# Scores of a tile in one run over four banks, in a fused adaLN block on one core

## The chip, the cores and the metric

One core of a Trainium2 chip runs the whole kernel, in one launch. The metric is the device time of an execution in microseconds: 976.61 us for the kernel before (median of 3 runs, 974.08 to 976.62). The core's engines each work through their own instructions in program order and meet at semaphores: TensorE (PE; its weight loads are PEld), VectorE (DVE), ScalarE (ACT), GpSimd (POOL) and SyncE (SP), which only issues DMAs here.

## What is computed

For x of 4 x 2048 tokens with 256 features (float32), with six modulation vectors per batch row from a small product:

```python
h = layernorm(x) * (1 + ca) + sa
q, k, v = phi(h @ Wq), phi(h @ Wk), h @ Wv     # phi = elu + 1, 16 heads of 16
S_t = S_{t-1} + k_t v_t^T ; z_t = z_{t-1} + k_t  # causal linear attention, a scan over tokens
x = x + ga * ((q_t S_t / max(q_t z_t, 1e-6)) @ Wo)
h = layernorm(x) * (1 + cb) + sb
x = x + gb * moe(h)   # 8 experts, top 2, capacity 1280 each, one shared silu layer of 512
```

## The kernel before, in words

The sequence is cut into 64 tiles of 128 tokens, four tiles to a group (16 groups). The attention phase is a software pipeline over slots, one tile to a slot (`slot_` of each engine; `run_slots` unrolls 8 slots to a loop body). Slot n handles tile n's scores, its state and its value products; the normalisation, the transpose and the out product of tile n-1; one quarter of the projections of the next group (q=0: transposes, q=1: Q, q=2: K, q=3: V, each of the last three in two halves, `stage1_qk` and `stage1_v`); and one step of the second layernorm and of the router for a group further back (q=0: transposes and logits, q=1: choice of experts, q=3: positions). q is the slot's place in its group. Every engine has its own order of these steps, written out by hand in its `slot_`; semaphores with running counts connect them.

Within one tile causal linear attention is a masked product. `scores` multiplies keys with queries, 32 rows (two heads, separated by a mask in QM) at a time: four row strips r = 0..3, each with two feature chunks cc. The scores of two strips (a pair) fill the tensor SCW, two PSUM banks of 512 columns, and DVE's `masked_scores` (L820) multiplies them with a triangle into Sm. The second pair uses the same two banks, so PE computes it (second call of `scores`) after DVE has read the first. PE's order in a slot (L1307 to L1360) is: scores of pair 0; logit rows, positions or h2 transposes, by q; `head_rows` (tile n-1's outputs transposed into bank MD); `key_rows` (keys transposed into bank MA); `from_state` (Q times the state, into OB); first half of stage 1; scores of pair 1; `attention_columns` (the normalised outputs An transposed into MA); `from_tile` part 0 (values times Sm, as column strips of 17 rows, adding to OB); `add_to_state`; second half of stage 1; `out_product` into MD; `from_tile` part 1. In a q=0 slot the logits stand before `from_tile` part 1 and `out_product`.

ACT's order in a slot (L656): OTs from OB of the last tile (L669), the masked queries of the next tile (L644), Kn from MA (L689), the first half of stage 1 (q=0: L582 drains both transposed halves; else L603 exp and L604 relu, or L652 for V), ATs from MA (L707), the layernorm rows (q=2 and q=3, L607), and the second half of stage 1. DVE's order (L964): mask of pair 0, `normalise_heads` (den, rden, An; L829 to L836), mask of pair 1, ATs' low part (L842), phi (L858) of the first half of stage 1, the state (L850), og = out product times ga (L1019), statistics; in q=1 phi of the second Q half and then the tails of both layernorms (L862 to L865), in q=2 phi of the second K half. Router steps of 0.2 to 0.7 us (`choose` in q=1, `place` in q=3) are put between these by `between`. POOL adds og to X (L491), applies the modulation in q=2 and q=3 (L459, L465), makes hT's low part in q=0 (L485) and sends the router's rows by indirect DMA (L475).

Projections, the out product and the expert products run as fp32r in three passes (`SPLIT`: high x high, high x low, low x high); for them w_o and ATs are kept as high and low parts. Scores, from_state, from_tile and the state run in full float32, where each matmul leaves two records in the trace.

Behind the attention phase (37 to 655 us of the span) stands a short end of the routing, and from 700 us on the expert phase, which uses SCW's two banks, MA and MD for its gate and down products and w_o's space for one of two XT buffers.

Of the kernel before, what the change touches and what calls it, by code (L numbers as in the profile page):

```python
# [21 lines left out]
P = 128  # L22
# [29 lines left out]
def adaln_block(nc, x, wqkv, wo, wr, wg, wd, c, wmod, out, xe, mod_rows):  # L52
    with ExitStack() as ctx:
# [24 lines left out]
        ATs = sb("ATs", [P, 2, DC, P], F32R)  # L78
        og = sb("og", [P, D])
        w_qkv = sb("w_qkv", [P, 2, DC, 3 * D], F32R)  # L80
        w_o = sb("w_o", [P, 2, DC, D], F32R)
# [62 lines left out]
        KS = sb("KS", [P, 2, DC, BW], F32R)  # L144
        w_d_lo = sb("w_d_lo", [P, FC, D], F32R)
# [11 lines left out]
        w_o_raw = Hf[:, DC * 3 * D:DC * 4 * D].rearrange("p (c n) -> p c n", c=DC)  # L157
# [16 lines left out]
              for a in (KS[:].rearrange("p k c n -> p (k c n)"), w_o[:].rearrange("p k c n -> p (k c n)"))]  # L174
# [46 lines left out]
        sc_full = sem("sc_full")  # L221
# [12 lines left out]
        at_hi = sem("at_hi")  # L234
        at_lo = sem("at_lo")
# [80 lines left out]
        def _(sp):  # L316
# [27 lines left out]
            sp.wait_ge(w_lo, 2)  # L344
# [206 lines left out]
        def _(act):  # L551
# [3 lines left out]
            for dst, src in ((w_qkv_raw, wqkv), (w_o_raw, wo), (w_r[:, :, 0:E], wr), (w_g_raw, wg)):  # L555
                act.dma_start(dst, src).then_inc(w_in, 16)
# [15 lines left out]
            for dst, src in ((w_qkv, w_qkv_raw), (w_o, w_o_raw)):  # L572
                act.activation(dst[:, 0], src, ACT.Copy).then_inc(w_hi, 1)
# [63 lines left out]
            def next_tile_queries(T, q, gp, tp, n):  # L637
# [3 lines left out]
                if n >= 1:  # L641
                    act.wait_ge(sc_full, 4 * T)
# [13 lines left out]
            def slot_(it, j, n):  # L656
# [47 lines left out]
                if tile_ok(n - 1):  # L704
                    act.wait_ge(at_full, T)
                    at_least(act, op_full, T - 1)
                    act.activation(ATs[:, 0].rearrange("p c i -> p (c i)"), MA[:, 0:D], ACT.Copy).then_inc(at_hi, 1)  # L707
# [76 lines left out]
        def _(dve):  # L784
# [5 lines left out]
            def early():  # L790

                for k, (dst, src) in enumerate(((w_qkv, w_qkv_raw), (w_o, w_o_raw))):
                    dve.wait_ge(w_hi, k + 1)
                    dve.tensor_tensor(dst[:, 1], src, dst[:, 0].bitcast(F32), ALU.subtract).then_inc(w_lo, 1)
# [15 lines left out]
                dve.wait_ge(w_hi, 3)  # L810
# [4 lines left out]
            def masked_scores(T, pair, tp, n):  # L815
                dve.wait_ge(sc_full, 4 * T + 2 * pair + 2)
                if pair == 0 and n >= 2:
# [3 lines left out]
                                  SCW[:].rearrange("p k (c w) -> p c k w", c=DC),  # L821
# [3 lines left out]
            def normalise_heads(T, between):  # L825

                on = MD[:].rearrange("p (h w) -> p h w", h=H)
# [10 lines left out]

            def attention_lo(T):

                dve.wait_ge(at_hi, T)
                dve.tensor_tensor(ATs[:, 1].rearrange("p c i -> p (c i)"), MA[:, 0:D],  # L842
                                  ATs[:, 0].rearrange("p c i -> p (c i)").bitcast(F32),
                                  ALU.subtract).then_inc(at_lo, 1)
# [119 lines left out]
            def slot_(it, j, n):  # L964
# [163 lines left out]
        def _(pe):  # L1128
# [17 lines left out]
            def scores(T, q, gp, tp, pair):  # L1146

                if isinstance(T, int) and T == 0 and pair == 0:
                    pe.wait_ge(gate_fix, 3)
                if pair == 0:  # L1150
                    pe.wait_ge(q_masked, 2 * T + 2)
                at_least(pe, sm_done, 2 * T + pair)
                last = [None, None]
                for cc in range(DC):
                    for k in range(2):
                        r = 2 * pair + k
                        rows = slice(32 * r, 32 * r + 32)
                        last[k] = mm(SC[k][:, cc * 2 * P:(cc + 1) * 2 * P], KT[rows, gp, cc, q * P:(q + 1) * P],  # L1158
                                     QM[rows, tp, :, cc, :], start=True, stop=True)
                for k in range(2):  # L1160
                    last[k].then_inc(sc_full, 1)

            def head_rows(T, q):

                pe.wait_ge(ot_done, T)
                at_least(pe, og_done, T - 1)
# [4 lines left out]
            def key_rows(T, q, gp):  # L1171
                at_least(pe, at_lo, T - 1)
# [12 lines left out]
            def from_tile(T, q, gp, tp, part):  # L1185

                pe.wait_ge(sm_done, 2 * T + 1 + part)
# [21 lines left out]
            def attention_columns(T, n):  # L1209
# [3 lines left out]
                else:  # L1213
                    pe.wait_ge(at_lo, T - 1)
# [24 lines left out]
            def stage1_qk(G, m):  # L1239
                N = G + 1  # L1240
                if isinstance(G, int) and N == 0 and m == 0:
                    pe.wait_ge(w_lo, 2)
# [23 lines left out]
            def h2_transposes(G, gn, hp):  # L1266
                pe.wait_ge(h2_done, 4 * (G - 1))
                if group_ok(gn):
# [25 lines left out]
            def positions(G, T, n):  # L1294
# [3 lines left out]
                at_least(pe, og_done, T - 1 if tile_ok(n - 2) else TILES)  # L1298
# [8 lines left out]
            def slot_(it, j, n):  # L1307
# [5 lines left out]
                if tile_ok(n):  # L1313
                    scores(T, q, gp, tp, 0)
# [142 lines left out]
```

## Time and profile before

| | |
|---|---|
| median of the runs | 976.61 us |
| the profiled execution | 978.2 us, its span 976.2 us |
| PE busy | 878.3 us (90%) |
| DVE busy | 652.8 us (67%) |
| ACT, POOL busy | 496.3 (51%), 514.9 us (53%) |
| slices 3 to 26 of 40, PE | nine tenths, PEclk 9 |

Times are microseconds from the start of the span. A row of the windows view is one stretch: its bounds, its length, then for PE, PEld, DVE, ACT and POOL the busy time and the number of instructions, then the granted clock of TensorE (1.00 is full), the DMA share and GB/s. A row of the groups by line is: line, engine, operation, output<-inputs, shapes, count; busy time of all together, mean ns of one; idle time ahead of them and what ended it. A row of the timeline is: start, duration, engine, line, operation, output<-inputs, shape and how many records were merged; in square brackets idle time before it and what ended it. A merged run of matmuls lasts until its last record has left the array, so the next run starts before it ends: PE's cost is read from start to start.

### The profile page before, as it was taken

To read this page: it belongs to the slowest core of one execution; us is meant where nothing else is said; L and a number is where in the kernel's file an instruction comes from. 1 tells how busy PE (TensorE), PEld (TensorE's weight loads), DVE (VectorE), ACT (ScalarE), POOL (GpSimd) and SP (SyncE) were. 2 spreads that over 40 slices of the span, in tenths; PEclk is the share of its full clock that TensorE was granted. 3 is DMA by queue.
4 is the path that set the end of the run, shared out by engine and by line. 5 is a ranking of instruction groups with operands and counts; after the bars stand their busy time and mean duration, and the time that the engine had idled before them with its cause. 6 is when DMAs were issued, how large, how long until landed. Compare 5 with 4: busy or idle time off the path is not lost. (4 is left out here: it accounts for less than half of the span.)

```text
span 976.2 us, 23383 instructions
## 1 busy us (share of the span) xinstructions
PE 878.3 (90%) x8232; PEld 736.6 (75%) x8232; DVE 652.8 (67%) x1869; ACT 496.3 (51%) x1002; POOL 514.9 (53%) x625
## 2 busy tenths in 40 slices
PE   4999999999999999999999999981099999999994
PEld 2777877777778777777777777761099999999994
DVE  4467587787877867778778787775056665665653
ACT  4555655655646555555565565432065555445541
POOL 3212445465554655556546555465625765566564
PEclk9899999999999999999999999995589999999997
DMA  9983012141231521302214112112156666666653
GB/s 318 335 272 97 16 31 110 23 131 66 66 116 13 130 86 43 127 31 82 78 21 96 40 37 60 33 39 64 53 148 147 143 131 141 144 138 141 129 110 43
DMA packets 70981, 98.36 MB, mean 101 GB/s; under 512 B 7794, under 2 KB 52850, under 8 KB 70792
## 3 DMA queue, kind: packets, MB, share of 16 engines
q1 hardware_dynamic: 37912, 52.09, 20.1%
q0 software_dynamic: 21760, 31.66, 14.6%
q10 hardware_dynamic: 11248, 13.81, 4.4%
q8 instruction: 37, 0.61, 0.3%
q14 instruction: 24, 0.20, 0.1%
HBM read 46.84 MB, written 63.36 MB: 113 GB/s over the span
## 5 line engine op out<-in xcount | busy, mean ns | idle before, releaser
L820 DVE TENSOR_TENSOR Sm<-SCW,tri 128x1024 f32<-128x1024 f32 x128 | 156.1, 1219 | 74.3 <-PE SCW L1158 74.3
L1158 PE MATMUL SCW<-QM,KT 32*128 32x256 f32 x1024 | 144.9, 400 | 10.5 <-DVE Sm L820 10.4
L475 POOL DMA_INDIRECT slot_rows<-Hrow,sloti x128 | 127.3, 994 | 45.1 <-issue 42.0
L533 POOL DMA_INDIRECT out<-EX,desti x80 | 126.6, 1583 | 29.6 <-issue 28.8
L491 POOL TENSOR_TENSOR X<-X,og 128x256 f32 (+1 forms) x64 | 47.3, 739 | 168.2 <-DVE og L1019 167.5
L1158 PEld LDWEIGHTS SCW<-QM,KT 32*128 32x128 f32 x1024 | 87.7, 184 | 45.8 <-issue 19.3
L1250 PE MATMUL PJ<-hT,w_qkv 128*128 128x512 f32 x384 | 106.9, 416 | 6.1 <-POOL hT L485 6.1
L485 POOL TENSOR_TENSOR hT<-N,hT 128x512 fp32r<-128x512 f32 x32 | 41.6, 1323 | 106.8 <-ACT hT L590 106.8
L603 ACT ACTIVATE EX<-PJ 128x512 f32<-128x512 f32 x64 | 38.2, 597 | 103.0 <-PE PJ L1250 103.0
L1250 PEld LDWEIGHTS PJ<-hT,w_qkv 128*128 128x128 f32 x384 | 69.6, 194 | 18.5 <-issue 6.3
L1191 PE MATMUL OB<-Sm,VA 128*17 128x128 f32 x2048 | 80.7, 275 | 0.0
L435 POOL TENSOR_TENSOR idle<-mhalf 128x1 f32<-128x1 f32 x100 | 33.2, 332 | 84.8 <-DVE EX L1103 59.2
L1019 DVE TENSOR_TENSOR og<-MD,MB 128x256 f32<-128x256 f32 x64 | 27.2, 424 | 67.8 <-PE MD L1224 67.8
L742 ACT ACTIVATE VA<-SCW 128x512 f32<-128x512 f32 x80 | 47.9, 598 | 40.9 <-PE SCW L1389 38.4
L1182 PE MATMUL OB<-QT,Sbd 128*128 128x128 f32 x512 | 67.6, 275 | 0.0
L1389 PE MATMUL SCW<-KS,w_g 128*128 128x256 f32 x480 | 63.2, 289 | 0.1
L1404 PE MATMUL MA<-w_qkv,QS 128*128 128x256 f32 x416 | 60.1, 281 | 3.0 <-DVE QS L1075 3.0
L1404 PE MATMUL MD<-w_qkv,hT 128*128 128x256 f32 x384 | 60.3, 281 | 2.5 <-DVE hT L1075 2.5
L1182 PEld LDWEIGHTS OB<-QT,Sbd 128*128 128x128 f32 x512 | 62.2, 192 | 0.0
L1389 PE MATMUL SCW<-w_o,w_g 128*128 128x256 f32 x480 | 62.2, 286 | 0.0
L1389 PEld LDWEIGHTS SCW<-KS,w_g 128*128 128x128 f32 x480 | 59.5, 194 | 0.5 <-DVE KS L1067 0.5
L1191 PEld LDWEIGHTS OB<-Sm,VA 128*17 128x17 f32 x2048 | 46.2, 97 | 17.6 <-issue 10.9
(191 smaller groups left out, 1996.3 us busy)
## 6 DMA issues: line engine op xcount, KB each, us to landing
Hrow<-slot_rows SPq DMA_DIRECT2D x32, 516.0 KB, 4.4
slot_rows<-erow ACTq DMA_DIRECT2D x1, 10400.0 KB, 53.1
X<-x SPq DMA_DIRECT2D x16, 512.0 KB, 4.3
out<-X SPq DMA_DIRECT2D x16, 512.0 KB, 3.0
Hrow<-mod_rows SPq DMA_DIRECT2D x16, 512.0 KB, 7.9
QT<-slot_rows SPq DMA_DIRECT2D x8, 516.0 KB, 3.7
slot_rows<-Hrow,sloti POOLq DMA_INDIRECT x128
N<-wd SPq DMA_DIRECT2D x4, 512.0 KB, 4.5
```

Of the source, the lines that this page charges most:

```text
L475: pool.indirect_dma_start(xe, bass.IndirectOffsetOnAxis(sloti[:, k, t:t + 1], 0), Hrow[:, 1 - gp, t, :], None, bounds_check=SLOTS - 1, oob ...
L485: pool.tensor_tensor(hT[:, 1, cidx, :], hT_raw[:, cidx, :], hT[:, 0, cidx, :].bitcast(F32), ALU.subtract).then_inc(h_lo, 1)
L491: pool.tensor_tensor(xt, xt, og[:], ALU.add).then_inc(x1_done, 1)
L533: pool.indirect_dma_start(out, bass.IndirectOffsetOnAxis(desti[s % 2][:, a:a + 1], 0), Ys[s % 2][:, a, :], None, bounds_check=TOK - 1, oob ...
L742: act.activation(hid_raw[s % 2][:, f, :], SC[hh].rearrange("p (f n) -> p f n", f=2), ACT.Silu).then_inc(silu_done, 1)
L820: dve.tensor_tensor(o.rearrange("p c (k w) -> p c k w", k=2), SCW[:].rearrange("p k (c w) -> p c k w", c=DC), tri[:].rearrange("p k i -> p ...
L1158: last[k] = mm(SC[k][:, cc * 2 * P:(cc + 1) * 2 * P], KT[rows, gp, cc, q * P:(q + 1) * P], QM[rows, tp, :, cc, :], start=True, stop=True)
L1182: mm(OB[:, i * P:(i + 1) * P], Sbd[:, 4 * i:4 * i + 4, :].rearrange("p h w -> p (h w)"), QT[:, gp, i // 2, q * P:(q + 1) * P], start=(i == ...
L1191: last = mm(OB[32 * a:32 * a + SW, i * P:(i + 1) * P], VA[:, gp, q, h, :], Sm[:, tp, h, :], start=False, stop=(part == 1), skip_group_chec ...
L1250: last = mm(PJ[m % 2][:], w_qkv[:, wp, cc, m * P:(m + 1) * P], hT[:, hp, cc, :], start=(cc + i == 0), stop=(cc == DC - 1 and i == len(SPLI ...
L1389: last = mm(SC[hh][:, (f % 2) * BW:(f % 2 + 1) * BW], w_g[:, wp, cc, f * P:(f + 1) * P], XT[par][:, xp, cc, :], start=(cc + i == 0), stop= ...
L1404: last = mm((MA, MD)[par][:, a * D:(a + 1) * D], hid[par][hp][:, f, a * P:(a + 1) * P], WD[k][wp][:, f, :], start=(f + i == 0), stop=(f == ...
```

## The change

SCW gets four banks: the first two are also MA and MD, the last two are SC[0] and SC[1]. `scores` runs once a slot, over all four strips; `masked_scores` is called twice at the head of DVE's slot. The transposes into MA and MD wait until the first masked pair has been read. The out product becomes one full float32 product (two matmuls) instead of six fp32r ones, so ATs and w_o lose their low parts; `attention_lo` goes, XT's second buffer is a new tensor VS, the router's positions move to PJ[1]. PE's slot is reordered. The core of the diff:

```diff
-        SCW = ctx.enter_context(nc.psum_tensor("SCW", [P, 2, 512], F32))
-        SC = [SCW[:, k, :] for k in range(2)]
+        SCW = ctx.enter_context(nc.psum_tensor("SCW", [P, 4, 512], F32))
+        MA, MD, *SC = (SCW[:, k, :] for k in range(4))
-        MA = ps("MA")
-        MD = ps("MD")
-        pos_ps = MD[:, 0:GT * E].rearrange("p (t e) -> p t e", t=GT)
+        pos_ps = PJ[1][:, 0:GT * E].rearrange("p (t e) -> p t e", t=GT)
...
-                act.activation(dst[:, 0], src, ACT.Copy).then_inc(w_hi, 1)
+            act.activation(w_qkv[:, 0], w_qkv_raw, ACT.Copy).then_inc(w_hi, 1)
...
                 if tile_ok(n):
                     masked_scores(T, 0, tp, n)
+                    masked_scores(T, 1, tp, n)
...
                 if tile_ok(n):
                     between()
-                    masked_scores(T, 1, tp, n)
                 between()
-                if tile_ok(n - 1):
-                    attention_lo(T)
                 between()
...
+            def scores(T, q, gp, tp):
+                pe.wait_ge(q_masked, 2 * T + 2)
+                at_least(pe, sm_done, 2 * T)
+                at_least(pe, og_done, T - 1)
+                at_least(pe, at_done, T - 1)
                 for cc in range(DC):
-                    for k in range(2):
+                    for r in range(4):
                         rows = slice(32 * r, 32 * r + 32)
+                        last = mm(SCW[:, r, cc * 2 * P:(cc + 1) * 2 * P], KT[rows, gp, cc, q * P:(q + 1) * P],
+                                  QM[rows, tp, :, cc, :], start=True, stop=True)
+                        if cc == DC - 1:
+                            last.then_inc(sc_full[r // 2], 1)
...
             def key_rows(T, q, gp):
-                at_least(pe, at_lo, T - 1)
+                pe.wait_ge(sm_done, 2 * T + 1)
...
             def out_product(T):
-                pe.wait_ge(at_lo, T)
+                pe.wait_ge(at_done, T)
                 for cc in range(DC):
-                    for i, (ap, wp) in enumerate(SPLIT):
-                        last = mm(MD[:, 0:D], ATs[:, ap, cc, :], w_o[:, wp, cc, :], start=(cc + i == 0),
-                                  stop=(cc == DC - 1 and i == len(SPLIT) - 1))
+                    last = mm(MD[:, 0:D], ATs[:, cc, :], w_o[:, cc, :], start=(cc == 0), stop=(cc == DC - 1))
```

`head_rows` waits for the first masked score of its slot too, `positions` for PJ[1] to be drained, `from_tile` part 0 in q=0 for the V projections to be drained. PE's slot after the change:

```python
                if tile_ok(n):
                    scores(T, q, gp, tp)
                ... # logit_rows (q=1), positions (q=3), h2_transposes (q=0), as before
                if tile_ok(n):
                    from_state(T, q, gp)
                if stage1:
                    ... # q=1: stage1_qk(G, 0); q=2: stage1_qk(G, 2); q=3: stage1_v(G, 0)
                if tile_ok(n - 1):
                    head_rows(T, n)
                if tile_ok(n):
                    key_rows(T, q, gp)
                    from_tile(T, G, q, gp, tp, 0)
                    add_to_state(T, q, gp, tp, j)
                if stage1 and q == 0:
                    stage1_transposes(G, gn)
                if tile_ok(n - 1):
                    attention_columns(T, n)
                if tile_ok(n):
                    from_tile(T, G, q, gp, tp, 1)
                if tile_ok(n - 1):
                    out_product(T)
                if stage1:
                    ... # q=1: stage1_qk(G, 1); q=2: stage1_qk(G, 3); q=3: stage1_v(G, 1)
                if q == 0 and group_ok(gn - 2):
                    logits(G, stage1)
```

The order of ACT's and DVE's other steps is not changed; ACT's copy of ATs now signals PE directly.

## Rows read from the trace of the kernel before

**Rows 1.** Windows view: the four slots of one group, q = 0 to 3.
```profile
306.23:315.31 9.08, 9.08 (x111) 7.30 (x107) 4.37 (x8) 6.49 (x13) 2.62 (x3) 1.00 0.00 0
315.31:324.89 9.58, 9.58 (x88) 7.28 (x87) 8.06 (x27) 3.82 (x9) 7.48 (x9) 1.00 0.53 193
324.89:335.31 10.42, 9.55 (x90) 7.19 (x87) 8.53 (x28) 6.37 (x15) 5.01 (x7) 1.00 0.66 117
335.31:345.60 10.29, 9.97 (x107) 8.16 (x104) 9.43 (x29) 5.72 (x14) 7.45 (x13) 1.00 0.04 9
```
**Rows 2.** Groups by line and shape: the column strips of `from_tile`, whole span.
```profile
L1191 PE MATMUL OB<-Sm,VA 128*17 128x128 f32 x2048 | 80.7, 275 | 0.0
```
**Rows 3.** Timeline of PE: one q=1 slot (its logit row left out).
```profile
315.31 1.13 PE L1158 MATMUL SCW<-QM,KT 32*128 32x256 f32 x8
...
316.53 0.60 PE L1168 MATMUL MD<-ident,OTs 128*128 128x128 f32 x4
316.97 0.38 PE L1174 MATMUL MA<-ident,KT 128*128 128x128 f32 x2
317.19 1.06 PE L1182 MATMUL OB<-QT,Sbd 128*128 128x128 f32 x8
318.00 1.65 PE L1250 MATMUL PJ<-hT,w_qkv 128*128 128x512 f32 x6
319.58 1.13 PE L1158 MATMUL SCW<-QM,KT 32*128 32x256 f32 x8
320.64 0.44 PE L1217 MATMUL MA<-ident,An 128*128 128x128 f32 x2
321.01 0.63 PE L1191 MATMUL OB<-Sm,VA 128*17 128x128 f32 x16
321.57 0.73 PE L1204 MATMUL SB<-VA,Kn 128*128 128x136 f32 x4
322.05 1.65 PE L1250 MATMUL PJ<-hT,w_qkv 128*128 128x512 f32 x6
323.54 0.87 PE L1224 MATMUL MD<-w_o,ATs 128*128 128x256 f32 x6
324.33 0.63 PE L1191 MATMUL OB<-Sm,VA 128*17 128x128 f32 x16
```
**Rows 4.** Timeline of PE: q=0's stage-1 transposes, q=2's second score run.
```profile
309.77 1.04 PE L1236 MATMUL PJ<-ident,N 128*128 128x128 f32 x8
...
330.00 1.13 PE L1158 MATMUL SCW<-QM,KT 32*128 32x256 f32 x8 [0.87 <-DVE Sm L820]
```
**Rows 5.** Timeline of ACT: drains and ATs in q=0, the drain behind q=1.
```profile
311.10 1.45 ACT L582 ACTIVATE N<-PJ,saca 128x512 f32<-128x512 f32 x2 [1.63 <-PE PJ L1236]
312.43 0.38 ACT L707 ACTIVATE ATs<-MA 128x256 fp32r<-128x256 f32 x1
...
323.74 0.60 ACT L603 ACTIVATE EX<-PJ 128x512 f32<-128x512 f32 x1 [2.23 <-PE PJ L1250]
324.23 0.59 ACT L604 ACTIVATE QT<-PJ 128x512 f32<-128x512 f32 x1
```
**Rows 6.** Timeline of DVE: from phi to mask to An, around q=2 and q=3.
```profile
325.52 0.69 DVE L858 SCALAR_TENSOR_TENSOR QT<-QT,EX 128x512 f32<-128x512 f32 x1
...
328.72 1.22 DVE L820 TENSOR_TENSOR Sm<-SCW,tri 128x1024 f32<-128x1024 f32 x1
...
330.35 0.42 DVE L836 TENSOR_TENSOR An<-MD,rden 128x256 f32<-128x256 f32 x1
...
335.53 1.22 DVE L858 SCALAR_TENSOR_TENSOR KT<-KT,EX 128x512 f32<-128x512 f32 x1
336.67 1.21 DVE L820 TENSOR_TENSOR Sm<-SCW,tri 128x1024 f32<-128x1024 f32 x1
...
340.70 0.41 DVE L836 TENSOR_TENSOR An<-MD,rden 128x256 f32<-128x256 f32 x1
```
**Rows 7.** Timeline of POOL: the add beside the phi at 335.53.
```profile
335.47 0.73 POOL L491 TENSOR_TENSOR X<-X,og 128x256 f32 x1 [4.97 <-DVE og L1019]
```

More of the change, by code:

```diff
@@ L77, in adaln_block @@
         An = sb("An", [P, H, DH])
-        ATs = sb("ATs", [P, 2, DC, P], F32R)
+        ATs = sb("ATs", [P, DC, P])
         og = sb("og", [P, D])
         w_qkv = sb("w_qkv", [P, 2, DC, 3 * D], F32R)
-        w_o = sb("w_o", [P, 2, DC, D], F32R)
+        w_o = sb("w_o", [P, DC, D])
         w_r = sb("w_r", [P, DC, 32])
@@ L173, in adaln_block @@
         XT = [a.rearrange("p (k c n) -> p k c n", k=2, c=DC)
-              for a in (KS[:].rearrange("p k c n -> p (k c n)"), w_o[:].rearrange("p k c n -> p (k c n)"))]
+              for a in (KS[:].rearrange("p k c n -> p (k c n)"), VS[:].rearrange("p k c n -> p (k c n)"))]
         Ys = [EXf[:, i * 512:(i + 1) * 512].rearrange("p (a n) -> p a n", a=2) for i in range(2)]
@@ L554, in _ @@
             act.wait_ge(wr_zero, 1)
-            for dst, src in ((w_qkv_raw, wqkv), (w_o_raw, wo), (w_r[:, :, 0:E], wr), (w_g_raw, wg)):
+            for dst, src in ((w_qkv_raw, wqkv), (w_o[:], wo), (w_r[:, :, 0:E], wr), (w_g_raw, wg)):
                 act.dma_start(dst, src).then_inc(w_in, 16)
@@ L706, in slot_ @@
                     at_least(act, op_full, T - 1)
-                    act.activation(ATs[:, 0].rearrange("p c i -> p (c i)"), MA[:, 0:D], ACT.Copy).then_inc(at_hi, 1)
+                    act.activation(ATs[:].rearrange("p c i -> p (c i)"), MA[:, 0:D], ACT.Copy).then_inc(at_done, 1)
                 if q == 2 and group_ok(gn - 1):
@@ L1144, in _, with head_rows @@
             pe.wait_ge(consts, N_CONST)
-            def scores(T, q, gp, tp, pair):
-                if isinstance(T, int) and T == 0 and pair == 0:
+            def scores(T, q, gp, tp):
+                if isinstance(T, int) and T == 0:
                     pe.wait_ge(gate_fix, 3)
[L1150 to L1153, printed above, removed]
+                pe.wait_ge(q_masked, 2 * T + 2)
+                at_least(pe, sm_done, 2 * T)
+                at_least(pe, og_done, T - 1)
+                at_least(pe, at_done, T - 1)
                 for cc in range(DC):
-                    for k in range(2):
-                        r = 2 * pair + k
+                    for r in range(4):
                         rows = slice(32 * r, 32 * r + 32)
[L1158 to L1163, printed above, removed]
+                        last = mm(SCW[:, r, cc * 2 * P:(cc + 1) * 2 * P], KT[rows, gp, cc, q * P:(q + 1) * P],
+                                  QM[rows, tp, :, cc, :], start=True, stop=True)
+                        if cc == DC - 1:
+                            last.then_inc(sc_full[r // 2], 1)
+            def head_rows(T, n):
                 pe.wait_ge(ot_done, T)
-                at_least(pe, og_done, T - 1)
+                if tile_ok(n):
+                    pe.wait_ge(sm_done, 2 * T + 1)
+                else:
+                    pe.wait_ge(og_done, T - 1)
                 for i in range(4):
@@ L1183, in from_state, with from_tile @@
                        QT[:, gp, i // 2, q * P:(q + 1) * P], start=(i == 0), stop=False, skip_group_check=True)
-            def from_tile(T, q, gp, tp, part):
+            def from_tile(T, G, q, gp, tp, part):
+                if q == 0 and part == 0:
+                    pe.wait_ge(pj_read, 6 * G + 6)
                 pe.wait_ge(sm_done, 2 * T + 1 + part)
@@ L1334, in slot_ @@
                         stage1_qk(G, 2)
-                    else:
+                    elif q == 3:
                         stage1_v(G, 0)
+                if tile_ok(n - 1):
+                    head_rows(T, n)
                 if tile_ok(n):
-                    scores(T, q, gp, tp, 1)
+                    key_rows(T, q, gp)
+                    from_tile(T, G, q, gp, tp, 0)
+                    add_to_state(T, q, gp, tp, j)
+                if stage1 and q == 0:
+                    stage1_transposes(G, gn)
                 if tile_ok(n - 1):
```

65 lines of the change are left out of this document (25 added, 40 removed).

## The prediction

> **What bounds the kernel now.** I read the busy share by slice first: PE at nine tenths through two thirds of the span, PEclk 9. Then four neighbouring slots of one group as windows [rows 1]: PE is busy for 9.08 of 9.08, 9.58 of 9.58, 9.55 of 10.42 and 9.97 of 10.29 us, at full clock (1.00, the 2.4 GHz level). The attention phase (37 to 655 us) is PE in program order, with a stall of size only in the third slot (q=2), where PE waits 0.87 for DVE's masked scores [rows 4], and 0.3 in the fourth. DVE is second: 8.06, 8.53 and 9.43 us of q=1, 2, 3. So the question is not only what PE saves, but whether DVE and ACT, both in program order, deliver in the order in which the new slot asks. The expert phase and its arithmetic are untouched. Below, S is the score run, q0 to q3 the four slots of a group; a number like "S+1.2" is counted from the slot's first score matmul.
>
> **PE's own work, part by part**, start to start in a q1 slot [rows 3]: S and the logit row 1.22 (the S alone 1.06, as the second one), head rows 0.44, key rows 0.22, from_state 0.81, first projection 1.58 (1.49 and 0.09 to enter the strips), second S 1.06, attention columns 0.37 (0.22 and 0.15 to leave for the column strips), from_tile 0.56, state 0.48, second projection 1.49, out product 0.79, from_tile 0.56: 9.58.
> The second S goes. Whether the merged S costs one run or two no row shows directly. Lower bound 1.06: two row strips run beside each other today (8 records of 256 columns in 1.06), and from_tile shows four column strips beside each other: 2048 records of 128 columns in 80.7 us busy, 39 ns each [rows 2], against 0.81/8 = 101 ns for full-array records of as many columns [rows 3]. Upper bound 2.12, two pairs in turn. I take 1.06: nearest are the four strips of from_tile, and each score strip again has a bank of its own.
> The Trainium skill (TensorE: Matmul & The Clock Gate, Measured speedup vs the span model) gives 3.07 times for four row strips; by it the run would be about 1.1 to 1.4. No run here shows it yet.
> Out product: six fp32r records of 256 columns take 0.79, about 0.12 each. Full f32 takes two records per matmul at half the rate (101 ns for 128 columns): 4 x 0.21 = 0.87. Bounds 0.75 to 1.0. Key rows now leave for column strips: +0.15. So a q1 slot without waits is 9.58 - 1.06 - 0.09 + 0.10 + 0.15 + 0.08 = 8.76, a saving of 0.8; q0 saves 1.0, as the state product no longer pays the entry to the logits' column strips. Were that all, 64 slots would give 52 to 58 us.
>
> **What waits now.** PE's edits are free of charge only if their inputs are there. Four places:
> *q1.* The merged S needs both masked scores of the last tile: long done. Head and key rows wait for the first masked score (sm0), the new users of its banks: S is followed by 2.3 us of from_state and projection and sm0 is ready near S+2.9; hidden. The state product waits for ACT's Kn with only from_tile (0.56) between; the key rows end, the copy takes 0.4, and it just fits; if not, 0.1. q1 = 8.8, **-0.8**.
> *q0.* The stage-1 transposes now stand right before the attention columns, but ACT still drains both transposed halves before it copies ATs. The transposes end at 309.77 + 1.04 = 310.81, ACT starts 0.29 later, reaches ATs after 1.33 and takes 0.38 [rows 4, 5]. With 0.05 to be seen, that is 2.05 after the transposes end, 2.22 after the attention columns start. PE has 0.37 + 0.56 = 0.93 to do. The out product waits 1.3, where two runs covered it before. q0 = -1.0 + 1.3 = **+0.3**. (The gated og, which S now waits for, lies beside the logits there, beside the second projection elsewhere; in a slot with neither, S waits 0.7 more.)
> *q2.* The second projection of q1 is now the last thing before S; it was followed by out product and from_tile (1.35 us, to the slot's end). ACT starts to drain it 1.69 after its start (322.05 to 323.74 [rows 3, 5]), that is S+0.1, and ends with QT at S+0.1+0.49+0.59 = S+1.2. DVE's phi of that QT can't start before, and everything up to the next sm0 is queued behind it on DVE: the two layernorm tails and two router steps, 325.52 to 328.72 = 3.2 us [rows 6]. So sm0 starts at S+4.4, where it started at S+3.8 (328.72 - 324.89). 1.28 after its start PE was released (328.72 to 330.00). Then it was for the second S, now it is for the head rows, at S+5.7. ACT's OTs copy, which from_state waits for, is late as well (behind the same drain, about S+1.8 against PE's S+1.1), but this wait of 0.7 runs out beside the longer one: 1.77 + 0.81 + 1.49 = 4.1 < 5.7. From there the rest costs 0.44 + 0.37 + 0.56 + 0.48 + 0.1 (An, at sm0 + 1.15 for the second mask + 2.05, from 328.72 to 330.77) + 0.37 + 0.56 + 0.87 + 1.59 = 5.35: q2 = 11.05, **+0.65**. The whole second S is swallowed.
> *q3.* Likewise phi of KT at S+1.2 (it ran at S+0.2, 335.53). It lasted 1.22 there against 0.69 for the same shape at 325.52, beside POOL's add at 335.47 [rows 6, 7]; I take 1.14, as POOL's modulation runs at that time: sm0 at S+2.4, it was S+1.36. From sm0 to the end of An were 4.44 us (336.67 to 341.11), which hold the router's steps; with the second mask in front 5.6, less 0.5 for one router step that no longer meets POOL: attention columns at S+7.5, and PE is there at S+6.2. Then 0.37 + 0.56 + 0.87 + 1.63: q3 = 10.9, **+0.6**.
> The Trainium skill (SBUF — State Buffer, SBUF: two separate sides) says that DVE and GpSimd hold a shared port pair exclusively for a whole instruction. The trace agrees: 1.22 against 0.69. By it each of these steps may come 0.5 earlier or later with the phase of POOL, a spread that stands in the range below.
>
> **The sum.** A full group changes by +0.3 - 0.8 + 0.65 + 0.6 = +0.75; there are 13 (groups 2 to 14): +10. Groups 0 and 1 have no router and group 15 no projections; their 12 slots save between 0 and 0.8 each, the latency chains bind some: I take 0.35, -4. At the start one ACT copy and one DVE subtraction of w_o go, about 0.5 of them on the path: -0.5. The subtraction of ATs leaves DVE (0.4 per slot), but DVE waits where it is late, so it gives nothing there. In all +5.5. The profiled execution took 978.2 (span 976.2), 1.6 above the median of 976.61: 983.7 in its terms, **982** in the median's.
>
> **Rivals.**
> *PE stays the bound* (faster). Were the waits hidden after all, the 52 to 58 us come out, less what q2 waits today: 922. For it: PE's busy share, and that DVE has 30 us of work in the four slots [rows 1], where PE would need some 35.5. Against it: an average hides that 3.2 us of DVE work stand between phi and sm0. Half way lies the case in which the waits are real but about 1 us a group shorter (DVE never meets POOL, the router steps in q3 cost 0.16 and not 0.6): -0.5 x 13 - 4.5 = -11: 965.
> *Much slower: the four strips don't run together.* Place: the merged S. Price: 1.06 more in every slot where nothing else is waited for, q0 and q1 fully, q2 and q3 hardly as sm0 and An come later than that anyway; some 34 slots: +34, 1018. It decides if strips share something that pairs don't. Against it: from_tile's four strips.
> *Masking becomes the bound.* The Trainium skill (TensorEngine Tiling, PSUM Bottleneck) warns that after such a speedup the copy out of PSUM may bind, on VectorE here. In this kernel, from rows: with both masks (2.3 us) ahead of the normalisation, An would be late in each slot, not only in q2 and q3. In q0 and q1 the chain ends at S+4.5 to 5.1 and PE asks at S+5.4, so it takes another 0.5 us of DVE delay to bind; then q0 and q1 cost 0.5 more each: +13, 995.
>
> **Chances.** My forecast with its own spread (980 to 1000, the 995 within it) 0.50; no change (974 to 979.5) 0.18; milder stalls, 955 to 973: 0.17; PE-bound, 915 to 955: 0.09; strips in turn, over 1000: 0.06. A measurement of this kernel can tell 0.3% (2.9 us) from nothing. The error of a walk through four slots, some 1 us a group, is 13 us in all, larger than the forecast's distance from zero, so same takes 0.18, slower 0.56 (the first and the last case) and faster 0.26. Range 951 to 1001.
>
> **What would show it.** Steps right: S as one run of 16 records in 1.1; no more than 0.9 between out product and what follows it; PE idle before the out product in q0 by 1.3 <- ACT ATs, before head rows in q2 by 1.5 or more <- DVE Sm, before attention columns in q3 by 1.3 <- DVE An; four slots like these 40.1 instead of 39.4 us long; PE's share down to about 85%, its clock still 1.00. Wrong: head rows in q2 released before S+5; An in q3 before S+6.5; S longer than 1.4; or a fall of the granted clock in these gaps, which no row lets me expect.

## The result, and the profile after

| | median us | runs | ratio to the kernel before (95%) |
|---|---|---|---|
| before | 976.35 | 4 (974.08 to 976.62) | |
| after | 989.35 | 4 (988.3 to 990.87) | 1.0126 [1.0097, 1.0155] |

The change makes the kernel 1.3% slower; 982 was forecast. The profiled execution of after took 990.16 (span 988.3), that of before 978.2 (span 976.2). A second set of the changed kernel, beside the last experiments, gave 985.94 (984.27 to 988.67), 1.0078 [1.0048, 1.0108].

The page of after, busy time and slices:
```profile
span 988.3 us, 23155 instructions
...
PE 835.8 (85%) x8104; PEld 696.6 (70%) x8104; DVE 627.8 (64%) x1804; ACT 484.9 (49%) x1001; POOL 509.6 (52%) x625
...
PE   4898998888898888888988889983089999999994
...
PEclk9899999999999999999999999997589999999997
```
PE lost 42 us of work and the span grew by 12: PE now stands idle in the middle of the span, where it had nines. From the first score run to the last, the profile of before takes 607.96 us, of which PE is idle for 15.5; that of after takes 621.76, with 71.6 idle. So this phase, in which the change lies but for 0.5 us at the start, is 13.8 longer, where 6 were forecast. Four slots of the same group as in [rows 1], as windows (us of the window, then each engine's busy time and count, granted clock, DMA):
```profile
314.88:324.60 9.72, 8.30 (x106) 6.50 (x105) 4.30 (x9) 6.07 (x13) 1.34 (x3) 1.00 0.00 0
324.60:333.33 8.73, 8.73 (x86) 6.69 (x86) 8.38 (x26) 3.49 (x9) 7.04 (x8) 1.00 0.50 181
333.33:344.40 11.07, 9.04 (x85) 6.54 (x85) 8.05 (x24) 6.07 (x13) 6.55 (x9) 1.00 0.42 130
344.40:355.29 10.89, 9.31 (x102) 7.59 (x101) 8.52 (x27) 6.00 (x15) 7.27 (x14) 1.00 0.06 13
```
The group took 39.37 and takes 40.41. Only q1 is PE-bound, and only q1 is shorter. The other three have 1.4, 2.0 and 1.6 us of idle PE, at full clock. Who ends these waits, over the whole span (idle time before the group, and its releaser, at the end of each line):
```profile
L1214 PE MATMUL SCW<-w_o,ATs 128*128 128x256 f32 x256 | 72.4, 405 | 17.1 <-ACT ATs L704 17.1
L1171 PE MATMUL OB<-QT,Sbd 128*128 128x128 f32 x512 | 72.2, 285 | 16.6 <-ACT OTs L666 16.5
L1157 PE MATMUL SCW<-ident,OTs 128*128 128x128 f32 x256 | 39.2, 275 | 17.2 <-DVE Sm L816 17.1
L1208 PE MATMUL SCW<-ident,An 128*128 128x128 f32 x128 | 25.9, 284 | 15.2 <-DVE An L832 15.2
```
Together 66 us. The kernel before had 10.4 us of such waits for DVE's masks and 4.4 for the router's positions; the work that PE lost is 42 us, where 52 to 58 were forecast. PE's timeline shows where they stand: out product of q0, from_state and head rows of q2, attention columns of q3 (its 0.40 for OTs at from_state isn't shown).
```profile
322.75 1.13 PE L1214 MATMUL SCW<-w_o,ATs 128*128 128x256 f32 x4 [1.28 <-ACT ATs L704]
323.81 0.64 PE L1276 MATMUL PJ<-h2T,w_r 128*32 128x128 f32 x16
324.60 1.15 PE L1144 MATMUL SCW<-QM,KT 32*128 32x256 f32 x16
325.68 0.33 PE L1283 MATMUL PJ<-ident,lgT 128*128 128x128 f32 x1
...
333.33 1.15 PE L1144 MATMUL SCW<-QM,KT 32*128 32x256 f32 x16
335.06 1.16 PE L1171 MATMUL OB<-QT,Sbd 128*128 128x128 f32 x8 [0.59 <-ACT OTs L666]
...
339.06 0.66 PE L1157 MATMUL SCW<-ident,OTs 128*128 128x128 f32 x4 [1.45 <-DVE Sm L816]
...
351.89 0.44 PE L1208 MATMUL SCW<-ident,An 128*128 128x128 f32 x2 [1.08 <-DVE An L832]
```
DVE in q2 and q3, which answers to [rows 6]:
```profile
334.55 0.69 DVE L847 SCALAR_TENSOR_TENSOR QT<-QT,EX 128x512 f32<-128x512 f32 x1 [1.36 <-ACT QT L600]
...
336.12 0.68 DVE L853 TENSOR_SCALAR nm<-mv 128x4 f32<-128x4 f32 x1
336.72 0.77 DVE L854 TENSOR_SCALAR vp<-mv 128x4 f32<-128x4 f32 x1
...
337.78 2.36 DVE L816 TENSOR_TENSOR Sm<-SCW,tri 128x1024 f32<-128x1024 f32 x2
...
345.62 0.92 DVE L847 SCALAR_TENSOR_TENSOR KT<-KT,EX 128x512 f32<-128x512 f32 x1 [1.74 <-ACT KT L600]
346.47 2.34 DVE L816 TENSOR_TENSOR Sm<-SCW,tri 128x1024 f32<-128x1024 f32 x2
...
348.80 0.73 DVE L951 COPY Hrow<-tokf 128x4 f32<-128x4 f32 x1
...
349.96 0.55 DVE L922 TENSOR_TENSOR pbase<-pbase,drop 128x32 f32<-128x32 f32 x1
...
350.51 0.65 DVE L924 TENSOR_TENSOR macc<-macc,msum 128x8 bf16<-128x8 bf16 x1
...
351.42 0.42 DVE L832 TENSOR_TENSOR An<-SCW,rden 128x256 f32<-128x256 f32 x1
```
The phi now starts at S+1.2 in both slots, 0.6 and 1.0 later than before: it waits 1.4 to 1.7 us for ACT's drain, where it waited for nothing. Everything behind it on DVE is late: the first masked score starts at S+4.45 in q2 and S+2.07 in q3, An at S+7.0 in q3.

The span by stretches: groups 2 to 13 +11.75 (0.98 each), group 14 +0.05, group 15 -0.6 and -3.0 behind its last S, group 0 +0.35, group 1 +2.2, the start +1.3: 12.1 in all. In group 1 the granted clock was at its half level for 3.4 us of q1, which then took 10.27 instead of 8.66; the second profile of the same kernel has those 3.4 us in group 0, so groups 0 and 1 together are equal in both (74.6), and so are groups 2 to 13. What makes one profile 4 us longer than the other (spans 988.3 and 984.2) lies ahead of the first S (1.2) and behind the last (2.7). Over the profiles of this and the next section, but for those of the set with the stall (told of at the very end), the first S stands at 36.3 to 38.5 us, and 320.6 to 331.6 us lie behind the last S, mostly the expert phase, whose work no kernel here changes. So neither the +1.3 nor the -3.0 can be put down to the change, and differences of a few us between medians say less than the lengths of slots.

### The profile page after: what moved, and what is told of

It reads as the page before. It is cut to its first block and busy times, and to the rows that moved or that the text cites. A ratio compares the mean times of both kernels' runs of the same rounds, so it can differ in the third digit from the quotient of the medians.

```text
span 988.3 us, 23155 instructions
## 1 busy us (share of the span) xinstructions
PE 835.8 (85%) x8104; PEld 696.6 (70%) x8104; DVE 627.8 (64%) x1804; ACT 484.9 (49%) x1001; POOL 509.6 (52%) x625
## 5 line engine op out<-in xcount | busy, mean ns | idle before, releaser
L816 DVE TENSOR_TENSOR Sm<-SCW,tri 128x1024 f32<-128x1024 f32 x128 | 150.3, 1214 | 33.1 <-PE SCW L1144 33.1
L686 ACT ACTIVATE Kn<-SCW 128x256 f32<-128x256 f32 x64 | 24.6, 384 | 141.2 <-PE SCW L1163 141.2
L1214 PE MATMUL SCW<-w_o,ATs 128*128 128x256 f32 x256 | 72.4, 405 | 17.1 <-ACT ATs L704 17.1
L1171 PE MATMUL OB<-QT,Sbd 128*128 128x128 f32 x512 | 72.2, 285 | 16.6 <-ACT OTs L666 16.5
L1144 PE MATMUL SCW<-QM,KT 32*128 32x256 f32 x1024 | 73.9, 402 | 5.2 <-DVE og L1006 3.8
L1006 DVE TENSOR_TENSOR og<-SCW,MB 128x256 f32<-128x256 f32 x64 | 27.2, 424 | 76.6 <-PE SCW L1214 76.3
L1214 PEld LDWEIGHTS SCW<-w_o,ATs 128*128 128x128 f32 x256 | 43.4, 189 | 34.9 <-ACT ATs L704 31.2
L1144 PEld LDWEIGHTS SCW<-QM,KT 32*128 32x128 f32 x1024 | 47.4, 185 | 24.2 <-issue 20.0
L1392 PE MATMUL SCW<-w_qkv,hT 128*128 128x256 f32 x384 | 61.7, 287 | 2.9 <-DVE hT L1062 2.9
L1392 PE MATMUL SCW<-w_qkv,QS 128*128 128x256 f32 x416 | 60.1, 281 | 2.0 <-DVE QS L1062 2.0
```

What stands on the lines that cost most here:

```text
L816: dve.tensor_tensor(o.rearrange("p c (k w) -> p c k w", k=2), SCW[:, 2 * pair:2 * pair + 2, :].rearrange("p k (c w) -> p c k w", c=DC), tr ...
L1144: last = mm(SCW[:, r, cc * 2 * P:(cc + 1) * 2 * P], KT[rows, gp, cc, q * P:(q + 1) * P], QM[rows, tp, :, cc, :], start=True, stop=True)
L1171: mm(OB[:, i * P:(i + 1) * P], Sbd[:, 4 * i:4 * i + 4, :].rearrange("p h w -> p (h w)"), QT[:, gp, i // 2, q * P:(q + 1) * P], start=(i == ...
L1214: last = mm(MD[:, 0:D], ATs[:, cc, :], w_o[:, cc, :], start=(cc == 0), stop=(cc == DC - 1))
L1392: last = mm((MA, MD)[par][:, a * D:(a + 1) * D], hid[par][hp][:, f, a * P:(a + 1) * P], WD[k][wp][:, f, :], start=(f + i == 0), stop=(f == ...
```

## The experiments

Four slots of an odd group (q0, q1, q2, q3), from one S to the next, in the profile of each kernel. Even groups have a q0 longer by 0.5 to 0.6 and nearly the same pattern (in the changed kernel their q2 is 0.2 shorter). Ratios are to the kernel before, which ran in the same set: 978.17 us in that of ATs first, OTs first, masks first and these three, 978.46 in that of the other rows.

| kernel | q0 | q1 | q2 | q3 | group | median us | ratio |
|---|---|---|---|---|---|---|---|
| before | 9.08 | 9.58 | 10.42 | 10.29 | 39.37 | | |
| changed | 9.72 | 8.73 | 11.07 | 10.89 | 40.41 | 985.94 | 1.0078 [1.0048, 1.0108] |
| ATs first | 8.48 | 9.30 | 9.96 | 10.89 | 38.63 | 967.43 | 0.9884 [0.9865, 0.9904] |
| OTs first | 9.71 | 8.73 | 11.05 | 10.87 | 40.36 | 996.84 | 1.0160 [1.0108, 1.0211] |
| masks first | 9.72 | 8.73 | 9.33 | 11.05 | 38.83 | 971.09 | 0.9921 [0.9893, 0.9948] |
| these three | 8.48 | 9.30 | 9.07 | 11.25 | 38.10 | 959.76 | 0.9808 [0.9769, 0.9847] |
| place late | 9.72 | 8.72 | 11.08 | 9.60 | 39.12 | 972.02 | 0.9947 [0.9918, 0.9976] |
| ATs, masks first, place late | 8.48 | 9.32 | 9.32 | 10.68 | 37.80 | 958.72 | 0.9802 [0.9775, 0.9829] |
| all four | 8.48 | 9.32 | 9.06 | 10.40 | 37.26 | 947.43 | 0.9674 [0.9641, 0.9708] |

**ATs first** (`e1_ats_first`). Theory: q0's wait is ACT's order alone.
```diff
                     act.activation(Kn[:, tp, :], MA[:, 0:D], ACT.Copy).then_inc(kn_done, 1)
+                if q == 0:
+                    copy_ats()
                 if stage1:
...
-                if tile_ok(n - 1):
-                    act.wait_ge(at_full, T)
...
+                if q != 0:
+                    copy_ats()
```


> The changed kernel with one move on ACT: in q=0 slots ATs is copied before the two transposed halves are drained. Theory (waits of the new order): the wait of 1.3 us ahead of the out product in q0 goes, but the hT subtraction on POOL, now 0.85 us early for the first Q projection, becomes late by about 0.5: q0 + q1 are 0.75 shorter, some 14 groups, -11 us: 978. Rival (each wait counts in full): -19, 970. Rival (these waits hang on something else): no change, 989.


q0 is 1.24 shorter: the 1.28 for ATs are gone, and 0.25 for ACT's drain of N, now behind ATs, are new. q0 and q1 together lose 0.67, where 0.75 were expected. But the kernel took 967.43, 22 under the first measurement of the changed one and not 11: q2 lost 1.1 too, which I had not asked for. DVE and POOL of this kernel around q2:
```profile
324.46 0.69 DVE L854 SCALAR_TENSOR_TENSOR QT<-QT,EX 128x512 f32<-128x512 f32 x1 [1.56 <-ACT QT L600]
...
325.56 0.16 DVE L861 TENSOR_SCALAR vp<-mv 128x4 f32<-128x4 f32 x1
...
326.58 2.36 DVE L823 TENSOR_TENSOR Sm<-SCW,tri 128x1024 f32<-128x1024 f32 x2
```
```profile
326.42 0.97 POOL L472 DMA_INDIRECT slot_rows<-Hrow,sloti  x1 [0.30 <-issue]
327.40 0.75 POOL L488 TENSOR_TENSOR X<-X,og 128x256 f32 x1
```
POOL's last send and its add now run beside the masks. In the changed kernel they ran beside the two tiny tail operations, which took 0.68 and 0.77 us there (336.12 and 336.72 above) and 0.16 here:
```profile
335.69 0.98 POOL L472 DMA_INDIRECT slot_rows<-Hrow,sloti  x1 [0.30 <-issue]
336.68 0.76 POOL L488 TENSOR_TENSOR X<-X,og 128x256 f32 x1
```
From phi to the mask it is 2.12 us instead of 3.23. So part of q2's loss was a matter of phase between DVE and POOL. q1's +0.57 is the price of q0's earlier end: part of it is PE waiting for POOL's hT (0.34).

**OTs first** (`e2_ots_first`): the copy of the out-rows that from_state waits for goes ahead of ACT's second-half drain of the slot before.
```diff
+                if stage1 and tile_ok(n) and q != 0:
+                    act.wait_ge(av_done, T + 1)
+                    at_least(act, on_full, T)
+                    act.activation(OTs[:].rearrange("p a i -> p (a i)"), OB[:], ACT.Copy).then_inc(ot_done, 1)
                 if stage1:
```


> The changed kernel with one move on ACT: in q=1, 2, 3 slots OTs is copied before the second projection half is drained, not after. Theory: the 0.6 and 0.4 us that PE waits for OTs ahead of from_state in q2 and q3 go, and come back as a longer wait for DVE's mask (q2) and An (q3); only groups 0 and 1 gain: -1 to -3 us, 987. Rival (waits add up): the 16.5 us that PE waits for OTs in the profile go, 973.


The waits for OTs are gone, and the slots keep their length to 0.02: as I had it, this wait ran out beside the later one. But seven slots of groups 4 to 13 took 12.3 to 12.5, and three of the four runs 995 to 998 us (the fourth 987.93). Windows and PE of one (q2, q3):
```profile
331.41:342.43 11.02, 8.96 (x85) 6.54 (x84) 7.99 (x24) 6.06 (x13) 6.50 (x9) 1.00 0.46 129
342.43:354.91 12.48, 10.74 (x102) 8.44 (x102) 8.50 (x27) 6.10 (x15) 7.29 (x14) 0.86 0.07 13
```
```profile
337.10 0.66 PE L1161 MATMUL SCW<-ident,OTs 128*128 128x128 f32 x4 [2.06 <-DVE Sm L820]
...
349.91 0.64 PE L1212 MATMUL SCW<-ident,An 128*128 128x128 f32 x2 [1.64 <-DVE An L836]
350.47 1.06 PE L1186 MATMUL OB<-Sm,VA 128*17 128x128 f32 x16
```
The same idle time stands in one piece of 2.06 (it was 0.59 and 1.45). In seven groups the clock is at its half level for 3.4 us. In three of them that begins 0.1 to 0.5 us behind the gap in q3, as here, and from_tile takes 1.06 instead of 0.63; in the other four it begins already in q2, 0.3 to 1.5 us behind the gap of 1.9 to 2.1. Some 1.5 us are lost each time, 11 in all. Shown is that it fell here and not in the same stretch of the changed kernel; why not in every group stays open.

**Masks first** (`e3_masks_first`): DVE's last phi of q1 and of q2 (the second Q and K half) go behind the next slot's masks; the layernorm tails stay in q1, behind its last router steps.
```diff
                     masked_scores(T, 1, tp, n)
+                if stage1 and q in (2, 3):
+                    phi(G, 2 * q - 3, npar)
...
-                    if stage1:
-                        phi(G, 1, npar)
...
-                if q == 2 and stage1:
-                    phi(G, 3, npar)
```


> The changed kernel with another order on DVE alone: in q=1 the layernorm tails and the last router steps come before phi of the second Q half, and that phi and the one of the second K half come after the masks of the next slot. Theory (phi waits for the late drain and holds the masks): the first mask of q2 starts at S+2.0 instead of S+4.45, of q3 at S+1.15 instead of S+2.07; q2 about 9.4 instead of 11.0, q3 9.9 instead of 10.9: -2.6 a group, -35 us: 954. Rival (DVE is simply too full with both masks ahead of the normalisation): its work is the same, so no more than -5: 984.


q2 is 9.33, as computed: the wait for DVE's mask is gone and 0.59 for OTs are left, so the queue ahead of the late mask was its loss. q3 isn't shorter (11.05, 9.9 expected): the first mask starts at S+1.2 now, and An still ends at S+7.6. DVE of this q3:
```profile
335.25 2.36 DVE L816 TENSOR_TENSOR Sm<-SCW,tri 128x1024 f32<-128x1024 f32 x2 [1.74 <-PE SCW L1144]
337.53 1.11 DVE L847 SCALAR_TENSOR_TENSOR KT<-KT,EX 128x512 f32<-128x512 f32 x1
338.56 0.69 DVE L950 TENSOR_SCALAR Hrow<-rk 128x4 f32<-128x4 f32 x1
...
339.75 0.53 DVE L922 TENSOR_TENSOR pbase<-pbase,drop 128x32 f32<-128x32 f32 x1
...
341.20 0.42 DVE L832 TENSOR_TENSOR An<-SCW,rden 128x256 f32<-128x256 f32 x1
```
The router's place steps stand between mask and An, and some of these operations (two are shown, 0.69 and 0.53 us for some 0.2) are stretched while POOL's modulation runs (to S+6.9). But the phi only changed places with the masks, and still stands ahead of An, so this run can't tell what the late phi costs q3. The profiled execution took 963.52; one more of the seven took 963.4, the other five 970 to 973.5. Its stretch behind the last S is the shortest of all, 320.6 us, and why five are longer stays open.

**These three** (`e4_all`).


> The three moves together. Theory: q0 8.5, q1 9.2 (with the hT wait), q2 9.0, q3 9.5: 36.2 a group against 40.6, -60 us: 930; PE busy near 95% again in the attention phase. Rival (DVE too full): 965 or more.


0.98 of before, but far from the 930 expected; q3 stays at 11.25, with 17 us of PE waiting for ACT's KT drain at the router's positions and 13 for An. That left one question for q3.

**Place late** (`e7_place_late`, and again as `e11_place_late_again` beside the changed kernel `e10_after_again`). The new theory: the place steps before An cost q3 its time.
```diff
+                between(False)
+                if tile_ok(n - 1):
+                    normalise_heads(T, between)
+                early_q3[0] = False
                 if q == 3 and group_ok(gn - 2):
...
                     place_ids(it, gp)
-                between(False)
-                if tile_ok(n - 1):
-                    normalise_heads(T, between)
```
(`early_q3` keeps the steps out of the normalisation of q3.)


> The changed kernel with q3's router place steps (place_ids and the place operations of VectorE) behind the quotient An instead of ahead of it. My theory: q3's An comes at S+7.4 because those steps are stretched beside POOL's modulation; An comes at about S+6.2, q3 goes from 10.9 to 9.6 or 9.7: -16 us, 973. Rival: the late phi and first masked score bind q3 whatever follows: 989. A third case: the gap moves and the granted clock falls in q3 in some groups, above 989.

> The router's place steps of q3 behind An, once more beside the changed kernel itself. In the first run q3 was 9.60 or 9.73 against the 10.89 of the changed kernel. My theory: -1.2 x 13 = -16 us against the changed kernel, whatever q1 does: 973 if q1 is 8.73. Rival: the gain in q3 is given back in q0 or q2 (stalls that only move): within 3 us of the changed kernel.

> The changed kernel itself, beside the two that follow, as their reference. In the four runs before this one every kernel, the one before too (1044.7), had 5 to 8 us added in the q1 slot of each group from group 3 on. If that condition is still there: about 989 + 65 = 1055 with q1 at 15 to 16; if it is gone: 989 with q1 at 8.73. In both cases q3 stays at 10.89.


The second run took 972.02 us, 13.9 less than the changed kernel beside it (973 and 16 expected); the changed kernel itself was without the stall, at 985.94. The first run stands in the set with the stall, at 1057.17. DVE of q3 (S at 338.11), second run:
```profile
339.33 0.90 DVE L847 SCALAR_TENSOR_TENSOR KT<-KT,EX 128x512 f32<-128x512 f32 x1 [1.75 <-ACT KT L600]
340.16 2.34 DVE L816 TENSOR_TENSOR Sm<-SCW,tri 128x1024 f32<-128x1024 f32 x2
...
343.60 0.42 DVE L832 TENSOR_TENSOR An<-SCW,rden 128x256 f32<-128x256 f32 x1
```
phi and mask are as late as in the changed kernel (S+1.2, S+2.05). An starts at S+5.5 instead of S+7.0, and q3 is 9.60, with 0.5 left of PE's waits (OTs, KT). Span 970.2 against 984.2, -14.0, nothing given back elsewhere. So the place steps in front of An are shown as a cause: without them the late phi makes PE wait for no An. They aren't shown as the only one. In the changed kernel DVE works without a gap from that phi (S+1.2) to An (S+7.0), and PE asks at S+6.4. Had the phi been 1.0 us earlier, as in the kernel before, the masks could have started at S+1.2, as they do in masks first, and not at S+2.07, and most of the 1.08 would have gone too; that is an estimate from these rows, and no run tried it.

**Pairs in turn** (`e5_pairs`). Is it the alternation of four strips that makes S one run's length?
```diff
-                for cc in range(DC):
-                    for r in range(4):
+                for pair in range(2):
+                  for cc in range(DC):
+                    for r in (2 * pair, 2 * pair + 1):
```


> The changed kernel with its score run split: pair 0 of strips first, pair 1 after it, everything else as changed. Each pair alone takes 8 x 0.12 = 0.97 us of issue, so S is about 2.1 us instead of 1.1. My theory: what four strips in one run save counts only in the slots whose S..out product is bound by TensorE, q0 and q1 (+1.06 each, sm0 of q2 and q3 wait for ACT and VectorE anyway and those waits swallow it): +2.1 x 14 groups = about +31 us, 1020. Rival, TensorE-bound everywhere: +4.2 x 16 = +68, 1057. Rival, the pairs never ran side by side: no change, 989.


S was not longer at all. PE of this kernel:
```profile
443.75 1.16 PE L1145 MATMUL SCW<-QM,KT 32*128 32x256 f32 x16
444.84 0.33 PE L1284 MATMUL PJ<-ident,lgT 128*128 128x128 f32 x1
```
1.09 to the next group, against 1.08 in the changed kernel. The records don't name their strip. But four of the sixteen start within 0.04 us and the next four 0.25 later, as in the changed kernel; in the kernel before, with two strips, only two start at a time. So the second pair's first ones start about 0.03 us after the first pair's, with the first pair's later ones still to come. Slots whose length no other condition touched are those of the changed kernel: q0 9.73, q3 10.89. The time itself, 1076.04 us, stands in the set with the stall. There it is 18.9 above place late; the changed kernel is 13.9 above place late in the last set. That leaves some 5 us for the order, of which the stall may be the cause, and not 31. So my expectation of +31 fell, and the rival that I priced at nothing stands, though not for its reason: the pairs do run side by side, whatever the order. What the change bought is that both pairs stand in one run with nothing between them. The order of the strips within it is free.

**Before, with only the plain f32 out product** (`e6_before_f32`).
```diff
-                    for i, (ap, wp) in enumerate(SPLIT):
-                        last = mm(MD[:, 0:D], ATs[:, ap, cc, :], w_o[:, wp, cc, :], start=(cc + i == 0),
-                                  stop=(cc == DC - 1 and i == len(SPLIT) - 1))
+                    last = mm(MD[:, 0:D], ATs[:, cc, :], w_of[:, cc, :], start=(cc == 0), stop=(cc == DC - 1))
```


> The kernel before with only the out product in plain f32 (no low parts of An, ATs and no third bf16 product). My theory, TensorE bound: the out product costs +0.08 x 64 = +5 us, 982. Rival: ACT's and VectorE's small copies of low parts were what delayed the out product, so their removal gives 0.4 us back in some slots: 970 or less.


1048.21 us in the set with the stall, ratio 1.0054 [1.0016, 1.0093], 2 to 9 us. But for the first, the slots of its profile ahead of the stall are 0.14 to 0.17 longer (9.64 for 9.49, 9.23 for 9.08), which for 60 slots gives some 9 us, an estimate. So this half of the change alone costs a PE-bound kernel more than the 0.08 a slot that I took, and no slot shows a gain from the copies it saves on ACT and DVE. In the changed kernel four f32 records take 0.78 before a projection, but 1.06 before the column strips of the logits (322.75 to 323.81 above), and in this one 1.06 before S; the six fp32r records of before took 0.79 before from_tile's column strips and 0.91 before S.

**ATs and masks first, place late** (`e8_best_a`, `e12_best_a_again`), **and OTs first with them** (`e13_best_b`).


> The changed kernel with three moves: ATs copied ahead of the two transposed halves (q0), the deferred features of VectorE behind the masks, and the place steps behind An (q3). If the three theories add: q0 8.5, q1 9.2, q2 9.3 (9.1 with the tails clear of POOL), q3 9.6: 36.6 a group against 40.4, about 941. Rival: q3's positions wait for KT's drain (17 us of such waits when all three earlier moves were together), q3 stays at 11: 961.

> ATs first, masks first and place late together, beside the changed kernel. My theory, the three add: q0 8.5 (9.0), q1 9.3, q2 9.1 to 9.3, q3 9.7 to 9.9, so -3.6 to -4 a group and -49 us against the changed kernel: about 941 without the added time of q1. Rival: what is saved in q3 comes back as a wait for KT's drain and q2 stays at the 10.25 of its first run: -25, 964.

> As the one before, and OTs copied ahead of ACT's second-half drain in q1 to q3. The waits of TensorE for OTs (16.5 us in the changed kernel) go and the drains come 0.6 later. Theory: TensorE is nearly bound in these slots now, so most of it is won: 4 to 8 us under the kernel without this move, about 935. Rival, from the run with OTs first alone: the waits merge into one longer gap and the granted clock falls in some groups: 5 us or more above it.


The first of these kernels came to 958.72 (941 expected; 1041.53 in its first run, in the set with the stall), with q0 to q2 as expected, but q3 at 10.68 and two slots at 12.2 with the clock down: for q3 the rival was right. An is no longer late, now PE waits for ACT's KT (1.20) and OTs (0.40), as ACT's four normalised rows, which waited 1.8 us for POOL, run ahead of the drain. With OTs ahead of the drain as well it is 947.43, 3.3% faster than before and 3.9% than the changed kernel. That is 11 us for the move which alone gained nothing; 4 to 8 were expected. Some 3 of them are the two falls of the clock, which the profile of the last kernel doesn't have in its groups 1 to 14. Four slots of this kernel, and PE in its q3:
```profile
295.21:303.69 8.48, 8.23 (x106) 6.46 (x105) 4.83 (x10) 5.27 (x11) 0.42 (x2) 1.00 0.00 0
303.69:313.01 9.32, 8.99 (x90) 6.75 (x86) 7.81 (x26) 4.46 (x11) 7.93 (x8) 1.00 0.44 159
313.01:322.07 9.06, 8.88 (x86) 6.62 (x85) 7.27 (x23) 4.57 (x10) 7.48 (x10) 1.00 0.38 142
322.07:332.47 10.40, 8.92 (x103) 7.51 (x102) 7.18 (x27) 7.59 (x19) 6.95 (x14) 1.00 0.16 38
```
```profile
324.69 0.19 PE L1307 MATMUL PJ<-mask,before 128*128 128x32 bf16 x1 [1.48 <-ACT KT L600]
```
q0 to q2 are within 0.2 to 0.35 us of PE's busy time. The 1.48 in q3 is what is left of the waits.

## Why the prediction was right, point by point

- *S as one run:* taken at 1.06, measured 1.08. The reason, four strips side by side, holds, and more widely than I had it (pairs in turn cost nothing). The estimate from the factor in the Trainium skill (TensorE: Matmul & The Clock Gate, Measured speedup vs the span model) was 1.1 to 1.4; the trace is just under its lower end.
- *q1:* 8.8, measured 8.73.
- *q0:* 9.38 for an odd group, measured 9.72. The wait is right (1.3, measured 1.28 <- ACT ATs, and shown by ATs first). Two other terms are not. PE's own part was to save 1.0 and saves 0.8 (busy 8.30 of the 9.08 before): I took out the entry into the logits' strips with the state product and did not put it back with the out product, which now stands there and takes 1.06 to the logits, not 0.87. And S's wait for the gated og, which I had beside the logits, shows: 0.14 us, in even groups 0.34 <- DVE og.
- *q2:* 11.05, measured 11.07 to 11.11 in odd groups and 10.9 in even ones (10.62 before); first mask S+4.4, measured S+4.45; head rows S+5.7, measured S+5.73. The step "everything behind phi is late on DVE" is shown by masks first (9.33). Of the 3.2 us between phi and mask, 1.1 are two tiny operations that meet POOL; I had carried them over from before without seeing them.
- *q3:* 10.9, measured 10.89; attention columns S+7.5, measured S+7.49. The chain that I added up, late phi, masks, router's steps, An, is the one in the trace. Two of its terms miss by 0.3 us each and cancel, which is luck: the first mask came at S+2.07, not S+2.4, and from its start to An's end it was 5.4, not 5.1. Place late shows that the router's steps in this chain were needed for the wait: with phi equally late q3 is 9.60, once they stand behind An. That the late phi was needed as well is worked out from the rows and not shown by a run.
- *The group:* +0.75 was forecast, +0.98 measured on average, the difference being mostly q0.
- *Groups 0, 1 and 15:* -4 was forecast, +2.0 measured; 1.6 of that is the stretch at half clock. This is the largest term that was wrong. What lies behind the last S came out at -3.0 and the start at +1.3 instead of -0.5, both within what profiles differ by. So the time moved the way that was forecast, but by 13.0 us and not by 5.4; that it didn't come out further off is in part the luck of those -3.0.
- *Rivals:* PE-bound: 71.6 us of idle PE in this phase speak against it. Strips in turn: against it 1.08. Masking as the bound: in q0 and q1 PE never waits for it. The milder stalls did not come by themselves, but their mechanism, DVE meeting POOL or not, is real: ATs first moved the phase and q2 gained 1.1.
- *The clock:* that it could fall in such gaps no row let me expect; in the changed kernel it did once in group 0 or 1, behind gaps of 0.5 to 1.4 us, and not in groups 2 to 14; with OTs first it did seven times there.

## What to carry to other kernels

Merging work on the bound engine pays only as far as the others deliver in the new order. List for each moved product the copy that it waits for, and what stands in front of that copy in its own engine's program: here four such moves on ACT and DVE turned 0.8% slower into 3.3% faster, in one set of runs. Two waits that end side by side must both go before either is worth something, and removing only the hidden one can cost time. A reordering that seems worthless by itself (OTs first) may be worth 11 us once the later wait is gone, so test it again at the end.

## What the runs showed of the hardware

- Matmuls on different row strips run side by side, whichever are issued first: 16 records of 256 columns on four strips take 1.08 to 1.09 us in either order, 8 on two strips took 1.06 [rows 3].
- Tiny DVE operations beside POOL's: 128x4 elements take 0.16 us alone and 0.68 to 0.77 beside a send or an add; some of the place steps, 0.14 to 0.2 alone, take 0.5 to 0.7 beside the modulation, others between them 0.17. The Trainium skill (SBUF — State Buffer, SBUF: two separate sides) has a shared port pair that a GpSimd operation, or a DVE one with two SBUF inputs or in a two-port mode, holds for a whole instruction. The trace agrees as far as times go; which of these operations are of that kind it doesn't show. For short operations the wait is several times the work.
- With a single gap of 1.9 to 2.1 us in PE per group and one of 1.5 to 1.7 behind it, the granted clock fell to half for 3.4 us in seven groups of ten; with gaps of 0.59 and 1.45, then 0.40 and 1.08, in none. Neither makes a rule: behind gaps of 1.2 and 0.40 it fell in two groups (ATs and masks first, place late), and behind one of 1.48 in q3 of the last kernel in none.
- Four runs (pairs, f32 alone, place late, the first best version) were made in one set on the chip of the first set, some 40 minutes later, and stood in another condition: the kernel before took 1044.7 (1036.99 to 1050.03, 19 runs) there, 978 in the set ahead of it and in the one behind it, which ran on another chip. The four took 1076.04, 1048.21, 1057.17 and 1041.53, ratios 1.0316 [1.0254, 1.0379], 1.0054 [1.0016, 1.0093], 1.0141 [1.0078, 1.0204] and 0.9972 [0.9937, 1.0006]. From group 3 on some slots are 3 to 8 us longer. In pairs and place late, PE, DVE and ACT stand still together for 3 to 5 us there; in f32 alone PE goes on in pieces, with gaps of 0.3 to 1.0 in which it waited for nothing that the profile shows. In q1 of one group of place late, DVE and then PE:
```profile
305.01 0.44 DVE L839 SCALAR_TENSOR_TENSOR Sbd<-SB,headmask 128x272 f32<-128x272 f32 x1 [3.98 <-issue]
```
```profile
306.18 2.07 PE L1218 MATMUL SCW<-w_o,ATs 128*128 128x256 f32 x4 [5.93 <-ACT ATs L704]
```
POOL issues its eight sends during this at the usual 1.28 us each. What the engines waited for, the records don't show; it stays open. The stall costs the kernels differently: place late is 1.4% slower than before in this set and 0.5% faster in the next. So ratios of this set don't carry over, and only slots outside the stall were compared.
